# A mixture kernel whose first half enters layer 1 only centred: deviations multiplied in later, half 1's masks on GpSimd

## What is computed

```python
def _layernorm(x, axis=-1, eps=1e-05):
    m = jnp.mean(x, axis=axis, keepdims=True)
    v = jnp.var(x, axis=axis, keepdims=True)
    return (x - m) / jnp.sqrt(v + eps)
...
    expert_ids = jnp.minimum(tid // tokens_per_expert, E - 1)
    for e in range(E):                       # E = 4
        g = jax.nn.silu(jnp.einsum('bsd,fd->bsf', hidden_states, Wg[e]))
        u = jnp.einsum('bsd,fd->bsf', hidden_states, Wu[e])
        y = jnp.einsum('bsf,df->bsd', g * u, Wd[e])
        out = jnp.where((expert_ids == e)[..., None], y, out)
...
    x = x + _L0_xattn_ref(_layernorm(x, axis=-1), itok_BxS_13_99985, ctx_2048, ctx_2048, ctx_2048)
    x = x + _L0_ffn_ref(_layernorm(x, axis=-1), L0_ffn_router_w, ...)
```

## Time and profile before

| | |
|---|---|
| median of 3 runs | 173.8 us (173.77 to 174.3) |
| the profiled execution | 173.89 us, of which the span of instructions is 171.8 us |
| PE busy | 166.6 us (97% of the span), 728 matmuls |
| DVE busy | 114.2 us (66%) |
| ACT busy | 67.8 us (39%) |
| POOL busy | 39.6 us (23%) |

### The profile page before, as it was taken

One profiled execution on the slowest core, in us unless ns is written; L12 is line 12 of the kernel. 1 busy time (PEld: TensorE's weight loads), 2 busy tenths in 40 slices (PEclk: granted clock), 3 DMA queues, 4 the chain that ended last, 5 costly groups with the idle time before them and its releaser, 6 DMA issues.

```text
span 171.8 us, 2194 instructions
## 1 busy us (share of the span) xinstructions
PE 166.6 (97%) x728; PEld 130.6 (76%) x728; DVE 114.2 (66%) x230; ACT 67.8 (39%) x112; POOL 39.6 (23%) x37
## 2 busy tenths in 40 slices
PE   6989999999999999999999999999999999999992
PEld 2568888888877888788787778788787887878881
DVE  0779778888984988588688528964744444444452
ACT  2472520551258254824664593152212222223320
POOL 2593000698200025539385000000000000000000
PEclk9999999999999999999999999999999999999999
DMA  4999000176400036742111200043361211100003
GB/s 137 307 373 352 23 4 2 25 236 227 122 0 4 15 130 181 203 160 67 61 61 61 61 0 4 8 126 126 113 195 45 75 65 61 62 0 4 2 0 122
DMA packets 7971, 16.41 MB, mean 95 GB/s; under 512 B 1336, under 2 KB 2200, under 8 KB 7832
## 3 DMA queue, kind: packets, MB, share of 16 engines
q1 hardware_dynamic: 7960, 16.27, 29.0%
HBM read 15.08 MB, written 1.18 MB: 95 GB/s over the span
## 4 chain that ended last, share of the span: by engine, by line
PE 97%; ACT 0%; POOL 0%; DVE 0%; issue 0%; DVEq 0%; POOLq 0%
PE bank L853 26%; PE bank L913 14%; PE bank L911 13%; PE bank L912 13%; PE bank L931 7%; PE bank L934 7%; PE bank L932 7%; PE bank L943 4%; PE bank L820 2%; PE bank L907 1%; PE bank L908 1%; PE bank L832 1%; ACT xn_hi L433 0%; POOL warm L383 0%; DVE xt L732 0%
## 5 line engine op out<-in xcount | busy, mean ns | idle before, releaser
L913 PE MATMUL bank<-xn_lo,gu_hi 128*128 128x512 f32 (+1 forms) x104 | 41.0, 394 | 0.0
L911 PE MATMUL bank<-xn_hi,gu_lo 128*128 128x512 f32 x96 | 37.9, 395 | 0.0
L912 PE MATMUL bank<-xn_hi,gu_hi 128*128 128x512 f32 x96 | 37.8, 394 | 0.0
L501 ACT ACTIVATE h_hi<-hid 128x512 fp32r<-128x512 f32 (+1 forms) x26 | 16.4, 632 | 45.7 <-DVE hid L720 45.7
L725 DVE TENSOR_TENSOR h_lo<-hid,h_hi 128x512 fp32r<-128x512 f32 (+1 forms) x26 | 20.2, 778 | 15.6 <-ACT h_hi L501 15.6
L913 PEld LDWEIGHTS bank<-xn_lo,gu_hi 128*128 128x128 f32 (+1 forms) x104 | 19.4, 186 | 5.0
L491 ACT ACTIVATE act_sb<-bank 128x512 f32<-128x512 f32 (+1 forms) x26 | 15.4, 594 | 18.1 <-PE bank L913 18.0
L398 POOL TENSOR_TENSOR gu_lo<-stage,gu_hi 128x512 fp32r<-128x512 f32 x12 | 17.9, 1516 | 17.6 <-ACT gu_hi L426 17.6
L912 PEld LDWEIGHTS bank<-xn_hi,gu_hi 128*128 128x128 f32 x96 | 18.0, 187 | 4.4
L911 PEld LDWEIGHTS bank<-xn_hi,gu_lo 128*128 128x128 f32 x96 | 18.0, 187 | 4.4
L931 PE MATMUL bank<-h_hi,wd_lo 128*128 128x512 f32 (+1 forms) x52 | 20.6, 396 | 0.0
(11 more groups left out here) (76 smaller groups left out, 213.1 us busy)
## 6 DMA issues: line engine op xcount, KB each, us to landing
stage<-gu_d SPq DMA_DIRECT2D x6, 512.0 KB, 3.5
stage<-wd_d SPq DMA_DIRECT2D x3, 512.0 KB, 4.1
x<-comb_d SPq DMA_DIRECT2D x8, 192.0 KB, 2.7
ids<-comb_d SPq DMA_DIRECT2D x8, 192.0 KB, 3.0
stage<-ctx_d SPq DMA_DIRECT2D x4, 256.0 KB, 5.0
xt<-xt_d SPq DMA_DIRECT2D x1, 1024.0 KB, 10.3
x<-comb_d SPq DMA_DIRECT2D x8, 128.0 KB, 3.1
ids<-comb_d SPq DMA_DIRECT2D x8, 128.0 KB, 2.8
```

Source lines behind the costliest of these rows:

```text
L911: nc.tensor.matmul(out[:], gu_lo[:, cols], xn_hi[:, h, k], start=(k == 0), stop=False)
L912: nc.tensor.matmul(out[:], gu_hi[:, cols], xn_hi[:, h, k], start=False, stop=False)
L913: ins = nc.tensor.matmul(out[0:rows, :], gu_hi[:, wide], xn_lo[:, h, k], start=False, stop=(k == KC - 1))
```

## The change

Half 0 is no longer normalised ahead of layer 1. Its tiles are only centred (x minus its mean): tiles 0 and 2 on DVE (statistics, aggregate, one subtraction), tiles 1 and 3 on ACT (a copy scaled by -1/256 whose accumulator gives minus the mean, then an addition of it as bias). As z is linear in x, the reciprocal deviation is multiplied in after the pick. For that PE transposes a column of `rstd`, repeated 128 times, for each of the four tiles into one bank ("rstd"), ACT copies the bank to `rstd_all`, and DVE multiplies `prod` of mixes 0 and 1 by it (`scale`). The statistics for the deviation of tiles 1 and 3 move behind `x_low`.

The warm-up falls from 20 to 8 matmuls of 512 columns, with 0, 2, 2, 1 matmuls of 256 columns ahead of the transposes of tiles 0 to 3 and three behind. Mix 0 is written out with its terms in another order: low weights late. The first transfer holds the identity and tiles 0 and 1; the separate identity transfer is gone. POOL's order becomes low parts 0 and 1, `rstd` of half 0, low parts 2 and 3, `rstd` of half 1, the three masks of half 1, then the rest. DVE's masks of half 1 are gone. DVE makes `xn_hi` block 1 of half 0, ACT block 0. `hidden_1` is cut into product, cast and low part; ACT makes the cast for blocks 0 and 2. `router_low_rows` moves from DVE to ACT.

```diff
-WARM_UP = 20
+WARM_UP = 8
...
-            sp.dma_start(x[:, 0:TT // 2], x_d[:, 0:TT // 2]).then_inc(x_in[0], 16)
-            sp.dma_start(x[:, TT // 2:TT], x_d[:, TT // 2:TT]).then_inc(x_in[1], 16)
+            sp.dma_start(first[:, 0:P + PAIR], first_d).then_inc(x_in[0], 16)
+            sp.dma_start(first[:, P + PAIR:P + 2 * PAIR], x_d[:, 0:PAIR]).then_inc(x_in[1], 16)
             load_piece(0)
-            sp.dma_start(consts_sb[:], consts_d).then_inc(consts_in, 16)
...
+            low_part(0)
+            low_part(1)
+            rstd_of(0)
+            low_part(2)
+            low_part(3)
+            rstd_of(1)
+            pool.wait_ge(ids_in, 16)
+            for e in range(1, E1):
+                nc.gpsimd.tensor_scalar(beyond[:, e - 1, HALF:], ids[:, HALF:], float(e * PER_EXPERT), None,
+                                        ALU.is_ge).then_inc(later_masks, 1)
...
+            def centre(t):                                            # ACT, tiles 1 and 3
+                act.wait_ge(x_in[t // (TT // 2)], 16)
+                nc.scalar.activation(xn[:, t], x[:, t], ACT.Copy, scale=-1.0 / D,
+                                     accum_out=minus_mean[:, t:t + 1]).then_inc(astep, 1)
+                act.wait_ge(astep, t // 2 + 1)
+                nc.scalar.activation(xn[:, t], x[:, t], ACT.Identity, bias=minus_mean[:, t:t + 1]).then_inc(normed_a, 1)
...
+            def spread_rstd():
+                act.wait_ge(side_done, side_at["rstd", 0, 0] + 1)
+                nc.scalar.activation(rstd_all[:], side_bank("rstd", 0, 0)[:], ACT.Copy).then_inc(rstd_in, 1)
...
-            apply_norm(0, range(TT // 2))
+            centre(1)
+            centre(3)
             high_part(0)
-            apply_norm(0, range(TT // 2, TT))
+            x_high("n1", 0, 0)
             high_part(1)
-            x_high("n1", 0, 0)
-            x_high("n1", 0, 1)
             high_part(2)
             high_part(3)
             first_z(0)
+            spread_rstd()
             apply_norm(1)
-            silu_z(0)
             first_z(1)
             x_high("n1", 1, 0)
             x_high("n1", 1, 1)
+            silu_z(0)
+            hidden_high(0)
             silu_z(1)
             first_z(2)
+            first_z(3)
             silu_z(2)
-            first_z(3)
+            hidden_high(2)
...
+            def centre(t):                                            # DVE, tiles 0 and 2
+                dve.wait_ge(x_in[t // (TT // 2)], 16)
+                tile_stats(0, t)
+                dve.wait_ge(dstep, steps[0])
+                step(nc.vector.bn_aggr(meanvar[:, 0, t], stats[:, t]))
+                dve.wait_ge(dstep, steps[0])
+                nc.vector.tensor_scalar(xn[:, t], x[:, t], meanvar[:, 0, t, 0:1], None, ALU.subtract).then_inc(normed_v, 1)
+            def scale(n):
+                dve.wait_ge(rstd_in, 1)
+                dve.wait_ge(z_picked, (n + 1) * (E1 - 1))
+                nc.vector.tensor_tensor(prod[:, n % 2], prod[:, n % 2], rstd_all[:], ALU.mult).then_inc(z_scaled, 1)
...
+            centre(0)
+            centre(2)
+            tile_stats(0, 1)
+            dve.wait_ge(side_done, side_at["n1", 0, 1] + 1)
+            nc.vector.tensor_scalar(xn_hi[:, 0, 1], side_bank("n1", 0, 1)[:], 1.0, None, ALU.mult).then_inc(xhi_done, 1)
             x_low("n1", 0, 0)
             x_low("n1", 0, 1)
+            tile_stats(0, 3)
+            layer_norm_vars(0, (1, 3))
             dve.wait_ge(x_in[2], 16)
             for t in range(TT):
                 tile_stats(1, t)
             layer_norm_vars(1)
-            masked = [thresholds(0)]
+            masked = [thresholds(0), None]
             pick(0, masked[0], [1])
             layer_norm_apply(1)
             pick(0, masked[0], [2, 3])
-            hidden_1(0)
+            scale(0)
+            pick(1, masked[0], [1, 2])
             x_low("n1", 1, 0)
             x_low("n1", 1, 1)
-            pick(1, masked[0])
-            hidden_1(1)
-            masked.append(thresholds(1))
+            hidden_product(0)
+            pick(1, masked[0], [3])
+            scale(1)
+            hidden_low(0)
+            hidden_product(1)
+            hidden_cast(1)
+            hidden_low(1)
             pick(2, masked[1])
...
+            def rstd_rows():
+                pe.wait_ge(powered, 1)
+                b = side_wait("rstd", 0, 0)
+                for t in range(TT):
+                    ins = nc.tensor.transpose(b[:, t * P:(t + 1) * P], rstd[:, 0, t:t + 1].to_broadcast([P, P]), consts_sb[:, 0:P])
+                ins.then_inc(side_done, 1)
...
+                pe.wait_ge(xhi_done, KC)
+                high(0)
+                weights_low(0, last=False)
+                high(1)
+                x_low(0, last=True)
+                x_low(1)
+                weights_low(1)
+                high(2)
+                x_low(2)
+                high(3)
+                x_low(3)
+                rstd_rows()
+                weights_low(2)
+                weights_low(3)
...
-            for _ in range(WARM_UP):
-                nc.tensor.matmul(bank[7][:], warm[:, 0:P], warm[:], start=True, stop=True)
-            pe.wait_ge(consts_in, 16)
-            norm_transposes("n1", 0, 0)
-            mix(0)
+            keep_warm(WARM_UP)
+            pe.wait_ge(x_in[0], 16)
+            norm_transposes("n1", 0, 0, (0, 2, 2, 1))
+            keep_warm(3, HALF // 2)
+            first_mix()
```

More of the change, by code:

```diff
@@ L60 @@
 SPREADS = 4
+PAIR = TT // 2 * D
 RING = HALVES * KC
@@ L440, in first_z, with apply_norm @@
                 nc.scalar.activation(prod[:, n % 2], ring_bank("z", n, 0)[:], ACT.Copy).then_inc(z_first, 1)
[L442 to L448, removed]
+            def centre(t):
[4 more added lines that the diff above has]
+                nc.scalar.activation(xn[:, t], x[:, t], ACT.Identity, bias=minus_mean[:, t:t + 1]).then_inc(normed_a, 1)
+            def apply_norm(n):
+                act.wait_ge(shifted, n)
+                what, hh = [("n1", 0), ("n1", 1), ("n2", 0)][n - 1]
+                act.wait_ge(side_done, side_at[what, hh, 1] + 1)
+                for t in range(TT):
                     if t not in BY_VECTOR[n]:
@@ L527, in _ @@
             high_part(8)
+            router_low_rows()
             first_z(5)
@@ L762, in _ @@
             add_block_1(4)
-            router_low_rows()
             pick(5, masked[1], [1])
@@ L812, in side_wait, with keep_warm, norm_transposes @@
                 return bank[b]
-            def norm_transposes(what, n, h):
+            def keep_warm(count, cols=HALF):
+                for _ in range(count):
+                    nc.tensor.matmul(bank[7][:, 0:cols], warm[:, 0:P], warm[:, 0:cols], start=True, stop=True)
+            def norm_transposes(what, n, h, between=()):
                 banks = [side_wait(what, h, k) for k in range(KC)]
                 for t in range(TT):
+                    if between:
+                        keep_warm(between[t], HALF // 2)
                     wait_normed(pe, n, t)
@@ L875, in mix, with first_mix, high, weights_low @@
                         between[e]()
+            def rstd_rows():
+                pe.wait_ge(powered, 1)
+                b = side_wait("rstd", 0, 0)
+                for t in range(TT):
+                    ins = nc.tensor.transpose(b[:, t * P:(t + 1) * P], rstd[:, 0, t:t + 1].to_broadcast([P, P]), consts_sb[:, 0:P])
+                ins.then_inc(side_done, 1)
+            def first_mix():
+                z = [ring_bank("z", 0, e)[:] for e in range(E1)]
+                f = slice(0, P)
+                def high(e):
+                    pe.wait_ge(w_hi, e + 1)
+                    for k in range(KC):
+                        nc.tensor.matmul(z[e], ctx_hi[:, e, k, f], xn_hi[:, 0, k], start=(k == 0), stop=False)
+                def weights_low(e, last=True):
+                    pe.wait_ge(w_lo, e + 1)
+                    for k in range(KC):
+                        ins = nc.tensor.matmul(z[e], ctx_lo[:, e, k, f], xn_hi[:, 0, k], start=False, stop=last and k == KC - 1)
+                    if last:
+                        ins.then_inc(z_done, 1)
+                def x_low(e, last=False):
+                    for k in range(KC):
+                        pe.wait_ge(xlo_done, k + 1)
+                        ins = nc.tensor.matmul(z[e], ctx_hi[:, e, k, f], xn_lo[:, 0, k], start=False, stop=last and k == KC - 1)
+                    if last:
+                        ins.then_inc(z_done, 1)
+                pe.wait_ge(xhi_done, KC)
[12 more added lines that the diff above has]
+                weights_low(3)
             def gate_or_up(g, up):
```

123 lines of the change are left out of this document (66 added, 57 removed).

## The result

The changed kernel takes 176.62 us (median of 4, 175.58 to 176.93), the kernel before 173.83. The ratio is 1.0144, 95% interval 1.0097 to 1.0191: slower by 1.4%, where 172.8 us was forecast. The profiled execution took 175.58 us, its span is 173.7.

A forecast was written before the change was run, and what follows sets the result against it. The prediction took a 9.71 us start and then a full tensor queue as the bound. From 173.89 us it took 1.23 for mix 1's earlier start and added 0.1 to 0.2 for the clock: 172.8 us, range 172.4 to 174.4.

The forecast's parts named there:

- The start: Up to mix 0's first matmul: power and shift leave the path, so it comes at 8.0 us against 9.71.
- Mix 1's start: The yardstick: 14.35 us instead of 15.58, 1.23 us earlier, with mix 0 paced by POOL.
- a term that I had called not binding: Weight loads in mix 0: piece 3 lands at 9.64 us, its high matmuls come at 11.9.
- Rival A: Start: tensor clock rises late, mix 0 starts near 9.05 us; a rise at 12 us gives 174.9. Chance 0.17.
- Rival B: Mix 2: POOL's masks hold DVE's `scale(0)`, PE waits up to 0.8 us for `x_low`; 173.3 to 173.7. Chance 0.15.
- my upper bound of 1.29: Half 1's masks on POOL: each comparison 0.8 us, between DVE's 0.42 and POOL's two-input row, 1.29.
- what must stay hidden: Work behind mix 1's start: all stays covered, `x_low` by 0.1 and 0.15 us, second norm's power by about 0.4.
- the row at 31.58: Earlier profile: DVE's `h_lo` took 1.54 us beside POOL's subtraction, against 0.69 for such a product alone.
- a wait that I did not see: Anywhere in the kernel: an unforeseen wait makes it slower, over 174.3 us. Chance 0.04.

The follow-up runs named there:

- the two moves of piece 8: Changed kernel with GpSimd's low part of piece 8 behind the second norm's power: 173.34 us; also waiting for layer 1's last hidden block: 172.50 us.
- the pause: Changed kernel with one wait more: GpSimd starts piece 8's low part only when the addition is done; 172.95 us, ratio 0.9952.
- old_middle: Changed kernel with the order around mixes 2 and 3 on ACT and DVE as before the change; 178.16 us, ratio 1.0252.
- the run again: The changed kernel measured again with no edit; 175.86 us, ratio 1.0101.
- cast_dve: Changed kernel with `router_low_rows` back on DVE behind the addition; 176.91 us.
- add_later: Changed kernel with mix 4's addition waiting for GpSimd's low part of piece 7, so asked for later; 176.68 us.
- places: Changed kernel with every tile shared with the kernel before at its old place in SBUF; 176.98 us.
- fenced: Changed kernel with piece 8's low part behind the second norm's power and waiting for layer 1's last hidden block; 172.50 us, ratio 0.9934.
- the streams alone: Kernel with only three streams of 12 GpSimd subtractions, four DVE additions beside each; no addition over 1.41 us, with loads, matmuls or ScalarE copies added 0.69 to 1.45.

## Why the prediction was wrong

**The start: right.** The first matmul of mix 0 was forecast for 8.0 us and came at 7.66; in the fifteen profiles with 8 warm-ups it came at 7.28 to 8.18. ACT's centring is 1.05 us a tile (0.54 up to the second pass, the accumulator's own 0.19 in it, and 0.51) where 1.0 was forecast; x landed at 3.98 us and not at 4.5, which covers the 0.34 us by which mix 0 came sooner.

**Mix 1's start: right in the middle, too sure of itself.** Forecast 14.35; 15.02 in the first profile, and 13.64 to 15.02 in the fifteen, median 14.45. Part of the spread is a term that I had called not binding: weight piece 1 landed at 8.9 us in the first profile (ACT idle for it 1.31 us), which pushed GpSimd's low parts and PE's low weights of expert 3.

**Rival A, a late clock in the start: came in a mild form, in six of the fifteen profiles.** In these six PE's first two transposes took 0.66 us, the pace of 1.2 GHz, in the other nine 0.41. Mix 0 then began at 7.79 to 8.18 us (7.28 to 7.69 in the nine), and mix 1 at 14.60 on average (14.18). So a late rise costs some 0.4 us. It came by 6.7 us at the latest, far from the 10 us from which the rival counts a loss.

**Rival B: right in kind, small where I put it, and the decisive thing elsewhere.** GpSimd's comparisons took 1.5 us each (4.63 for three), over my upper bound of 1.29. `scale(0)` took 1.06 us beside them instead of 0.69, and half 1's `xn_lo` came about 0.3 us late for PE. The Trainium skill (GPSIMD Engine Reference, Key points) states that DVE instructions with two SBUF inputs contend with GpSimd. By that rule, the trace agrees in these 1.06 us. Taking the masks away gave nothing.

**The step that failed** is the paragraph on what must stay hidden. It followed GpSimd's low parts 4 to 8, 0.9 us later than before, only to the second norm's power on GpSimd's own queue, and did not ask which DVE instructions with two SBUF inputs stand beside them. The addition of mix 4 does, and the x1 transposes wait for it. It could bear 1.2 us over its 0.69. From the row at 31.58 I had the price of a hold as the rest of one GpSimd instruction, at most 0.85 us; by that price the place was safe. The price was wrong: a hold can last as long as GpSimd's stream, here 3.2 us over the addition's own time, which put 2.0 us on the path. The moves of the change put more of the stream behind PE's need: its last subtraction ends at 42.97 us, 1.45 behind PE's being ready, where before it was 42.15 against 41.82. They do not by themselves explain the hold, since in the kernel before the addition was let in beside the same stream. All that the prediction had for this was a chance of 0.04 for a wait that I did not see.

**And a second bill that no rival had.** Of the 29 runs with the hold, 19 had a mean clock of 0.990 or less; of the 26 without it (the two moves of piece 8 and the pause), none. By kernel: 12 of the 21 runs of those with 8 warm-ups and a wait of 2.0 to 2.1 us in the profile had the fall, 3 of 4 with 20 warm-ups, and all four of old_middle, whose profile has a wait of 3.7 us. My rival A looked for a thin tensor queue at the start; a plain wait of 2 us in the middle did it. The fall itself cost 1.5 us in the run again. The 12 runs with it lie 1.9 us above the other nine on average (176.65 against 174.77), and the rest has a reason in the start. In the eleven profiles with 8 warm-ups and a wait of 2.0 to 2.1 us, the four with the fall (again, cast_dve, add_later, places) are just the four with the late rise of the clock, 0.66 us for the first two transposes; the seven with 0.41 have no fall. What ties a late rise at 6 us to a fall at 44 us no run here shows.

**Sum.** Without the hold the change is worth 0.66% (fenced), 1.0 us, as forecast (173.8 less 172.8). That the number of the start came out so well is in part luck, since mix 1's start alone moves by 1.4 us from profile to profile. The wait of 2.0 us turns the gain into a loss of 1.0: 174.8, where the nine runs without the fall have 174.77. The fall adds 1.5 us and the late start that goes with it some 0.4, which makes 176.7, where the twelve have 176.65. The median of 176.62 is that of four runs of which three had the fall.

**Open.** Why DVE's addition to xt is not let in at a boundary, when the kernel before and the streams alone let it in, and other instructions in the same trace are. Changed one at a time, these did not end the hold: the instruction behind it, its place in the stream, transfers, addresses, the masks, the writing in place, the order of its inputs, the predicated copy ahead. Matmuls or ScalarE beside the streams alone did not bring it about. What did end it was a pause of GpSimd. A combination of two causes is not ruled out. I also did not show what decides whether the clock falls behind a wait of 2.0 us.

## What to carry to other kernels

When an engine's stream moves against another's, list for every stretch which DVE instructions with two SBUF inputs now stand beside GpSimd, and cost each as if held until GpSimd's stream pauses, not to its next instruction. If one of them releases TensorE, give GpSimd a wait there: one semaphore was worth some 3 us here. And do not count a wait of TensorE in the middle of a kernel at its length alone, since the clock may be lost behind it: here 2.0 us of waiting cost 3.5 in the runs with the fall.

## What the runs showed of the hardware

A comparison on GpSimd, 512 int32 columns to uint8, takes 1.49 us (three in 4.63, with the gaps between them), more than its two-input f32 subtraction (1.29), and 3.6 times DVE's 0.42.

A DVE addition of 512 columns with two SBUF inputs, 0.69 us alone, is let in beside back-to-back subtractions of GpSimd at the next boundary in some places (1.10 us in the kernel before) and held to the end of the whole row in others (2.92, 3.90 and 6.20 us); in the three kernels in which GpSimd's last low part was moved or made to wait, the same addition took 1.44 to 1.45 us.

ScalarE's accumulator costs an instruction of its own, 0.19 us, behind the 0.42 of the copy.

When TensorE's clock rises at the start varies from run to run of almost the same program. The first eight transposes in the run again, in its timeline, pass at the pace of 1.2 GHz (0.66 and 0.63 us for two) and then at that of 2.4 (0.38), with the change between 5.7 and 6.4 us; in the first profile they take 0.38 to 0.41 from 5.2 us on. The granted clock reads 1.00 in both stretches. Six of the fifteen profiles with 8 warm-ups show the late rise.

```profile
4.81 0.66 PE L891 MATMUL bank<-first,xn 128*128 128x128 f32 x2
5.69 0.63 PE L891 MATMUL bank<-first,xn 128*128 128x128 f32 x2
6.41 0.38 PE L891 MATMUL bank<-first,xn 128*128 128x128 f32 x2
```
